# A twelve-layer perceiver on one core: layer 3 in three bfloat16 parts, unread products in layer 9, rows of norms between last steps

## The reference, cut to what matters

```
x = x + _L0_xattn_ref(_layernorm(x), ctx, ctx, ...)     # layer 1
x = x + _L0_attn_ref(_layernorm(x), ...)                # layer 2
x = x + _L0_ffn_ref(_layernorm(x), k0, k1, k2, s0, s1, s2)   # layer 3
...
x = x + _L2_ffn_ref(_layernorm(x), Wc, bc, W1, b1, W2, b2)   # layer 9
...
def _L0_ffn_ref(x, k0, k1, k2, s0, s1, s2):             # kernels are booleans: +1 or -1
    h = concatenate([x, -x])                            # 256 wide
    h = relu(s0 * (h @ pm1(k0))) * 2                    # 512 wide
    h = relu(s1 * (h @ pm1(k1))) * 2                    # 512 wide
    return s2 * (h @ pm1(k2))                           # 128 wide

def _L2_ffn_ref(x, Wc, bc, W1, b1, W2, b2):             # 32 experts x 4 sets, per batch of 32 rows
    logits = einsum('bntd,des->bntes', grouped, Wc) + bc + tie
    perm = (logits == max over the 32 rows)
    permuted = einsum('bntd,bntes->bnesd', grouped, perm)
    inner = relu(einsum('bnesd,esdf->bnesf', permuted, W1) + b1)
    result = einsum('bnesf,esdf->bnesd', inner, W2) + b2
    return einsum('bnesd,bntes->bntd', result, perm)
```

## Time and profile before

| | us |
|---|---|
| median of 3 runs | 3016.36 |
| lowest and highest | 3015.51, 3020.53 |
| the profiled execution, its own time | 3021.84 |
| its span in the trace | 3020.1 |
| PE busy | 2791.3 (92%) |
| DVE busy | 1734.3 (57%) |
| ACT busy | 1310.7 (43%) |
| POOL busy | 709.3 (23%) |
| layer 3, from the close of layer 2 to its own | about 743 to 836 |
| layer 9 | about 1461 to 1546 |

### The profile page before, as it was taken

How to read it: one execution, slowest core, us unless ns; L and a number is a source line. 1 busy time by engine, 2 the same in 40 slices (tenths; PEclk the granted TensorE clock), 3 DMA queues, 4 the chain that set the end, 5 groups by cost and what they waited for, 6 DMA issues and landing times.

```text
span 3020.1 us, 68763 instructions
## 1 busy us (share of the span) xinstructions
PE 2791.3 (92%) x26391; PEld 1793.0 (59%) x26391; DVE 1734.3 (57%) x5652; ACT 1310.7 (43%) x3546; POOL 709.3 (23%) x1552
## 2 busy tenths in 40 slices
PE   8999999897989979998689987789999999999898
PEld 7888885555467756665467765444444444444465
DVE  6778777665178877569558876722233232332544
ACT  4556564452278852348448874311121121111321
POOL 2444440000068850024027761000000000000000
PEclk9999999999999999888679998889999999999999
DMA  5111110000021110320011122040000000000000
GB/s 135 46 49 45 48 39 9 2 2 6 0 62 51 49 26 3 89 87 2 5 49 42 42 66 99 2 138 1 1 1 1 1 1 1 1 1 1 1 1 15
DMA packets 125902, 92.01 MB, mean 30 GB/s; under 512 B 41283, under 2 KB 122566, under 8 KB 124230
## 3 DMA queue, kind: packets, MB, share of 16 engines
q1 hardware_dynamic: 125574, 87.61, 10.2%
HBM read 83.89 MB, written 3.67 MB: 29 GB/s over the span
## 4 chain that ended last, share of the span: by engine, by line
PE 56%; DVE 8%; issue 6%; ACT 2%; DVEq 2%; POOLq 0%; POOL 0%; ACTq 0%
PE banks L3462 25%; PE banks L927 3%; PE banks L911 2%; PE banks L898 2%; PE banks L936 2%; PE banks L3885 2%; PE banks L3876 2%; PE banks L3874 2%; PE banks L3517 1%; PE banks L2390 1%; DVE probs L1099 1%; PE banks L900 1%; PE banks L3472 1%; PE banks L899 1%; PE banks L2006 1%
## 5 line engine op out<-in xcount | busy, mean ns | idle before, releaser
L1012 ACT ACTIVATE probs<-probs,nbias 128x257 f32<-128x257 f32 x512 | 254.4, 502 | 0.0
L1228 POOL TENSOR_SCALAR probs<-probs,rinv 128x257 f32<-128x257 f32 x512 | 238.5, 485 | 24.5 <-DVE rinv L1110 21.2
L3462 PE MATMUL banks<-Wz,hT 128*64 128x256 f32 x2048 | 226.4, 379 | 0.0
L3462 PE MATMUL banks<-Wn,hT 128*64 128x512 f32 x1024 | 225.4, 593 | 0.0
L3462 PE MATMUL banks<-Wr,hT 128*64 128x512 f32 x1024 | 225.2, 592 | 0.0
L3735 POOL COPY rb<-hT 128x512 f32<-128x512 f32 x32 | 35.8, 1118 | 801.5 <-ACT hT L3538 777.3
L3462 PEld LDWEIGHTS banks<-Wz,hT 128*64 128x64 f32 x2048 | 147.2, 137 | 87.5 <-issue 18.3
L3704 DVE TENSOR_TENSOR pr<-hb,banks 128x512 f32<-128x512 f32 x32 | 22.0, 688 | 298.3 <-PE banks L3517 298.3
L718 POOL TENSOR_SCALAR probs<-probs,rinv 128x257 f32<-128x257 f32 x256 | 120.6, 485 | 203.6 <-DVE rinv L658 203.0
L3462 PEld LDWEIGHTS banks<-Wr,hT 128*64 128x64 f32 x1024 | 73.6, 137 | 132.5 <-issue 127.9
L3462 PEld LDWEIGHTS banks<-Wn,hT 128*64 128x64 f32 x1024 | 71.0, 137 | 129.5 <-issue 129.5
(11 more groups left out here) (647 smaller groups left out, 6450.6 us busy)
## 6 DMA issues: line engine op xcount, KB each, us to landing
kvT<-in_ctx_T SPq DMA_DIRECT2D x192, 128.5 KB
kv<-in_ctx SPq DMA_DIRECT2D x64, 128.0 KB
kv<-in_ctx SPq DMA_DIRECT2D x32, 256.0 KB
W<-in_L_ffn_W_T SPq DMA_DIRECT2D x2, 2048.0 KB
Wr<-in_L_ffn_w_hh_T SPq DMA_DIRECT2D x1, 4096.0 KB
Wn<-in_L_ffn_w_hh_T SPq DMA_DIRECT2D x1, 4096.0 KB
Wz<-in_L_ffn_w_hh_T SPq DMA_DIRECT2D x1, 4096.0 KB
v_last<-v_last SPq DMA_DIRECT2D x192, 8.0 KB, 1.6
```

The source lines that it names most:

```text
L1012: i = e.activation(s, s, ACT.Exp, bias=self.nbias[v][:, r:r + 1], scale=self.scale, accum_out=self.rows_sum[v][:, r:r + 1])
L1228: e.tensor_scalar(s, s, self.rinv[v][:, r:r + 1], 1.0, ALU.mult, ALU.mult)
L3462: mm = e.matmul(self.bank[b][hf * BATCH:(hf + 1) * BATCH, 0:n], lhs, rhs, start=start, stop=stop, tile_position=(0, hf * BATCH))
```

## The change

Layer 3: the +1/-1 weights of the first two products become bfloat16, and each float32 operand is taken in three bfloat16 parts whose sum it is: its own upper half, read in place as every second 16-bit element (`high`); the upper half of what is left (`rest`, float32); and what is then left (`low`, bfloat16). DVE makes `rest` and `low` with two subtractions (`split`), for the turned rows (once a round) and for each of the four column groups of the first product's result. A call becomes three bfloat16 calls into one bank. The third product stays float32. The order on PE, ACT and DVE is written out anew: the first product of a round runs ahead of the second of the round before it, the third later; the last quarter's statistics stand ahead of the parts of the hidden rows, its rows between those of rounds 0 and 1.

Layer 9: the gathered columns are copied in one instruction for each bank (3 on ACT, 1 on DVE a group, 512 columns each); three float32 products of 512 columns into bank 6, which nobody reads, stand before the first pair, and one of 128 columns into bank 2 ahead of each `expert_pe`.

Layers 1, 7, 8: `next_rows` of quarters 0, 1, 2 go one by one between or behind the last steps.

```diff
-            if g == UN - 2:
-                for q in range(3):
-                    self.next_rows(e, q)
+            if g >= UN - 3:
+                self.next_rows(e, g - UN + 3)
...
+    FC, ROUNDS, TURN_BANKS, PARTS = 4, NT // 4, (0, 1, 2, 7), 3
...
-        self.W = [self.sb(f"W{n}", [P, c * wd]) for n, c, wd in ((0, 2, 512), (1, 4, 512), (2, 4, 128))]
+        self.W = [self.sb(f"W{n}", [P, c * wd], dt) for n, c, wd, dt in ((0, 2, 512, BF16), (1, 4, 512, BF16), (2, 4, 128, F32))]
         self.h = [[self.sb(f"h{n}", [P, FC * R4]) for n in range(2)] for _ in range(2)]
+        self.y_rest, self.y_low = [self.sb("y_rest", [P, R4]) for _ in range(2)], [self.sb("y_low", [P, R4], BF16) for _ in range(2)]
+        self.h_rest, self.h_low = [self.sb("h_rest", [P, FC * R4]) for _ in range(2)], [self.sb("h_low", [P, FC * R4], BF16) for _ in range(2)]
...
+        self.y_split, self.h_split = self.sig("y_split", N), self.sig("h_split", FC * N)
...
+    def high(self, t):
+        return t.bitcast(BF16).rearrange("p (n two) -> p n two", two=2)[:, :, 1]
+    def split(self, e, x, rest, low):
+        e.tensor_tensor(rest, x, self.high(x), ALU.subtract)
+        e.drain()
+        return e.tensor_tensor(low, rest, self.high(rest), ALU.subtract)
+    def parts(self, x, rest, low):
+        return self.high(x), self.high(rest), low
+
     def pe(self, e):
         self.norm_pe(e, (0, 1, 2))
+        self.first(e, 0)
+        self.first(e, 1)
+        self.second(e, 0)
+        self.norm_pe(e, (3,))
+        self.first(e, 2)
+        self.third(e, 0)
+        self.second(e, 1)
+        self.first(e, 3)
+        self.third(e, 1)
+        self.second(e, 2)
+        self.second(e, 3)
+        self.third(e, 2)
+        self.third(e, 3)
+    def first(self, e, r):
         self.signs_ready.wait_ge(e, 1)
+        self.y_split.wait_ge(e, r + 1)
+        at = slice(r * R4, (r + 1) * R4)
+        parts = self.parts(self.prog.yT[:, at], self.y_rest[r % 2][:, :], self.y_low[r % 2][:, :])
+        for c in range(self.FC):
+            self.n_yT.wait_ge(e, max(r, c % 2) + 1)
+            self.relu0.wait_ge(e, self.FC * r + c - 1)
+            for n, part in enumerate(parts):
+                i = e.matmul(self.bank[c % 2][:, :], self.W[0][:, c * P:(c + 1) * P], part, start=n == 0, stop=n == 2)
+            i.then_inc(self.mm0.up(), 1)
+    def second(self, e, r):
         FC = self.FC
...
+        self.signs_ready.wait_ge(e, 3)
+        self.n_yT.wait_ge(e, 3)
+        of = lambda t, k: t[r % 2][:, k * R4:(k + 1) * R4]
+        h0 = [self.h[n][0] for n in range(2)]
+        for c in range(FC):
+            self.relu1.wait_ge(e, FC * r + c - 1)
+            for k in range(FC):
+                self.h_split.wait_ge(e, FC * r + k + 1)
+                for n, part in enumerate(self.parts(of(h0, k), of(self.h_rest, k), of(self.h_low, k))):
+                    i = e.matmul(self.bank[2 + c % 2][:, :], self.W[1][:, k * 512 + c * P:k * 512 + (c + 1) * P], part,
+                                 start=k == 0 and n == 0, stop=k == FC - 1 and n == 2)
+            i.then_inc(self.mm1.up(), 1)
+    def third(self, e, r):
+        FC, h1 = self.FC, self.h[r % 2][1]
+        self.relu1.wait_ge(e, FC * (r + 1))
+        self.x_done.wait_ge(e, r - 1)
+        for s in range(4):
             for c in range(FC):
+                i = e.matmul(self.bank[4 + r % 2][:, s * P:(s + 1) * P], h1[:, c * R4 + s * P:c * R4 + (s + 1) * P],
+                             self.W[2][:, c * P:(c + 1) * P], start=c == 0, stop=c == FC - 1)
+        i.then_inc(self.mm2.up(), 1)
     def act(self, e):
...
+        self.relu_first(e, 0)
+        self.norm_act_std(e)
+        self.relu_first(e, 1)
+        self.relu_second(e, 0)
+        self.norm_act_yT(e, (3,))
+        self.relu_first(e, 2)
+        self.relu_second(e, 1)
+        self.relu_first(e, 3)
+        self.relu_second(e, 2)
+        self.next_root(e, 0)
+        self.next_root(e, 1)
+        self.relu_second(e, 3)
+        self.next_root(e, 2)
+    def relu_first(self, e, r):
+        FC, h0 = self.FC, self.h[r % 2][0]
+        for c in range(FC):
+            self.mm0.wait_ge(e, FC * r + c + 1)
+            self.mm1.wait_ge(e, FC * (r - 1))
+            self.h_split.wait_ge(e, FC * (r - 1))
+            e.activation(h0[:, c * R4:(c + 1) * R4], self.bank[c % 2][:, :], ACT.Relu, scale=self.scales[:, 0:1]).then_inc(self.relu0.up(), 1)
+    def relu_second(self, e, r):
+        FC, h1 = self.FC, self.h[r % 2][1]
+        self.signs_ready.wait_ge(e, 3)
+        self.mm2.wait_ge(e, r - 1)
+        for c in range(FC):
+            self.mm1.wait_ge(e, FC * r + c + 1)
+            e.activation(h1[:, c * R4:(c + 1) * R4], self.bank[2 + c % 2][:, :], ACT.Relu, scale=self.scales[:, 1:2]).then_inc(self.relu1.up(), 1)
+    def split_rows(self, e, r):
+        self.n_yT.wait_ge(e, r + 1)
+        self.mm0.wait_ge(e, self.FC * (r - 1))
+        self.split(e, self.prog.yT[:, r * R4:(r + 1) * R4], self.y_rest[r % 2][:, :], self.y_low[r % 2][:, :]).then_inc(self.y_split.up(), 1)
+    def split_hidden(self, e, r):
         FC = self.FC
...
+        self.mm1.wait_ge(e, FC * (r - 1))
+        for c in range(FC):
+            at = slice(c * R4, (c + 1) * R4)
+            self.relu0.wait_ge(e, FC * r + c + 1)
+            self.split(e, self.h[r % 2][0][:, at], self.h_rest[r % 2][:, at], self.h_low[r % 2][:, at]).then_inc(self.h_split.up(), 1)
+    def add_x(self, e, r):
+        x = self.prog.X[:, r * R4:(r + 1) * R4]
+        self.mm2.wait_ge(e, r + 1)
+        e.scalar_tensor_tensor(x, self.bank[4 + r % 2][:, :], self.scales[:, 2:3], x, ALU.mult, ALU.add).then_inc(self.x_done.up(), 1)
+        e.drain()
+        if r < 3:
+            self.next_statistics(e, r)
     def dve(self, e):
...
         e.tensor_scalar(self.W[0][:, :], self.raw[0][:, :], 2.0, -1.0, ALU.mult, ALU.add)
         e.drain()
         e.tensor_tensor(self.W[0][:, 0:512], self.W[0][:, 0:512], self.W[0][:, 512:1024], ALU.subtract).then_inc(self.signs_ready.up(), 1)
+        self.split_rows(e, 0)
         e.tensor_scalar(self.scales[:, 1:3], self.scales[:, 1:3], 2.0, None, ALU.mult).then_inc(self.signs_ready.up(), 1)
         for n in range(1, 3):
             e.tensor_scalar(self.W[n][:, :], self.raw[n][:, :], 2.0, -1.0, ALU.mult, ALU.add)
         e.drain().then_inc(self.signs_ready.up(), 1)
...
+        self.split_rows(e, 1)
+        self.norm_dve_statistics(e)
+        self.split_hidden(e, 0)
+        self.norm_dve_rows(e)
+        self.split_hidden(e, 1)
+        self.split_rows(e, 2)
+        self.split_hidden(e, 2)
+        self.add_x(e, 0)
+        self.split_rows(e, 3)
+        self.split_hidden(e, 3)
+        self.add_x(e, 1)
+        self.next_rows(e, 0)
+        self.next_rows(e, 1)
+        self.add_x(e, 2)
+        self.next_rows(e, 2)
+        self.add_x(e, 3)
...
         for step in range(NT + 5):
-            if step == NT + 3:
-                self.next_rows(e, 0)
-                self.next_rows(e, 1)
-            if step == NT + 4:
-                self.next_rows(e, 2)
...
             if t >= 0 and t % 4 == 3 and t < 12:
                 self.x_added.wait_ge(e, t + 1)
                 self.next_statistics(e, t // 4)
+            if step == NT + 1:
+                self.next_rows(e, 0)
+            if step == NT + 2:
+                self.next_rows(e, 1)
+            if step == NT + 4:
+                self.next_rows(e, 2)
...
                 if t > 4 and t % 4 == 1:
                     self.x_added.wait_ge(e, t - 1)
                     self.next_statistics(e, t // 4 - 1)
-                if t == NT - 2:
-                    for q in range(3):
-                        self.next_rows(e, q)
+                if t > NT - 4:
+                    self.next_rows(e, t - NT + 3)
 
     def rotary(self, e, t, b, ts, bs, bank):
         bq = lambda t: t.rearrange("p (b q) -> p b q", q=SEQ)
...
                         i = e.matmul(bank[2 + b][:, at], p.y[lo:lo + SEQ, g * R4 + s * P:g * R4 + (s + 1) * P],
                                      self.pick_tok[g % 2][lo:lo + SEQ, at], start=True, stop=True)
                 i.then_inc(self.gather_mm.up(), 1)
+        self.keep_warm(e, bank[6][:, :], 3)
         self.G_dve.wait_ge(e, 4)
         self.G_act.wait_ge(e, 4)
...
+    def gathered(self, g, b):
+        return self.G3[:, :, 16 * g:16 * g + 16].rearrange("p x (s b) -> p x s b", b=BPT)[:, :, :, b]
+    def keep_warm(self, e, bank, times):
+        for _ in range(times):
+            e.matmul(bank, self.prog.ones[:, :], self.prog.y[:, 0:bank.shape[1]], start=True, stop=True)
+
...
     def expert_pe(self, e, n):
+        self.keep_warm(e, self.bank[2][:, 0:P], 1)
         self.inner_ready.wait_ge(e, n + 1)
         self.G_back.wait_ge(e, n)
         for k in range(2):
...
             if phase == 2:
                 self.gather_mm.wait_ge(e, g + 1)
                 for b in (1, 2, 3):
-                    for s in range(4):
```

(21 more changed lines are left out.)

44 lines of the change are left out of this document (1 added, 43 removed).

## The result

The changed kernel takes 3001.03 us (median of 4 runs, 2995.86 to 3001.28), the kernel before 3018.18 beside it: a ratio of 0.9931, 95% interval 0.9910 to 0.9953, or -20.8 us (-27 to -14). In six more runs on another chip it is 0.9922 (0.9901 to 0.9944), -23.6. The profiled execution has its own time of 3000.97 and a span of 2999.2, against 3021.84 and 3020.1.

The account below looks back on a forecast made before the run. PE's turns bound layer 3; PE and DVE waiting on each other at half clock bound layer 9's pairs. -15.5 - 0.4 + 1.5 - 7.8 - 0.6 - 1.5 - 0.9 = -25.2 us: 2996.6, median 5.5 lower, 2991.2; range 2983 to 3005.

Parts of the forecast that it names:

- rival 1: Layer 9: PE's clock falls back in the pairs, unread products wake nothing; -14.6 us in all, 3001.8; chance 0.26.
- the start of the pairs: Layer 9 before the first pair: regrouped copies -0.4 us for four groups, three unread products +1.5 us.
- the pairs: Layer 9's loop: clock held at 1.00, period 1.52 instead of 2.02 us, -7.8 us; first `inner_pe` another -0.6.
- the spread part: Layer 9 behind the pairs: the raised clock lasts into it, where it was at half clock; -1.5 us.
- the rows: Rows moved between last steps: layer 1 -0.3, layer 8 -0.6, layer 7 0 us; -0.9 in all.
- Layer 3, the products: Three bfloat16 parts cost 0.651 us a call, not 0.869; second product saves 13.9 us, first about 1.3.
- rival 3: Layer 3: reads of every second 16-bit element go at half rate, layer 3 +14.6 us; 3027 in all; chance 0.07.
- Layer 3, order and start: Layer 3 as a whole, by a hand timeline of the new order and DVE's splits: -15.5 us (-18 to -12).
- 3.1 of stalls: Layer 3: PE's 0.78 us wait for the last Relu before each third product goes, once a round; 3.1 us.
- The timeline: Layer 3: first product at 746.4, PE full from 765.2, last add at 819.2 instead of 835.22.
- Rival 2: Layer 9: regrouped copies are quick as well, -4.2 us more, -29.9 in all, 2986.5; chance 0.12.
- Rival 4: Layer 3's gains are covered by something unseen, as DVE held up by both operands; about 3013; chance 0.05.

Follow-up runs that it names:

- l3_order: Changed kernel with layer 3 in its new order but in float32, without splits: -13.0 us (-18 to -8) against the kernel before.
- more_unread: Changed kernel plus unread products before the first turn of seven layers and ahead of layer 9's spread part: -1.8 us (-7 to +3) against the kernel before.
- no_unread: Changed kernel without any unread product in layer 9: -23.9 us (-31 to -17) against the kernel before.
- no_unread_again: Changed kernel without any unread product in layer 9, run once more: -23.3 us (-30 to -17) against the kernel before.
- l9_only: Kernel before with only layer 9's copies and unread products changed: -12.1 us (-18 to -6) against the kernel before.
- no_three: Changed kernel without the three unread 512-column products ahead of layer 9's pairs: -17.2 us (-24 to -11) against the kernel before.

## Why the prediction was right, and where it was not

The forecast was 2991 with -25.2 us; it came to 3001, with -20.8 and -23.6. Faster was right, and inside layers 3 and 9 so was the mechanism. The number is no witness for it: rival 1's 3001.8 lies nearer to 3001.03 than the forecast, and only the period of 1.57 at clock 1.00 rules it out. Nor does the near sum: layer 3 and the start of the pairs came out some 2.5 us better than forecast, the pairs, the spread part and the rows 3.1 worse, and these cancel.

- **Layer 3, the products.** A bfloat16 record turns every 0.227 us on `h`, 0.225 on `h_rest` and 0.215 on `h_low`, so a call takes 0.667 where 0.651 was forecast (13.9 + 1.3 = 15.2 for both products forecast, 13.2 measured by l3_order). The parts read at a step are 5% slower than the dense one, so rival 3 (0.33 and above) is out. Here a page of the Trainium skill (Advanced Engine Details and Errata, SBUF Cachelines) agrees to within these 5%: its two hits on a line are met by a step of one element in 4 bytes.
- **Layer 3, order and start.** -15.5 forecast, -16.9 measured. The order alone gave 3.7, where 3.1 of stalls were counted. A split is 0.75 + 0.61 = 1.36 (1.37 forecast). The timeline held: with the 3.6 added by which it was ahead, the trace of after has the first product at 746.8 (746.4 by hand), the first split of `h` at 750.8 (751.2), the last add at 818.35 (819.2). Too much were those 0.85 at the end and the 0.5 that I took off for a start at half clock.
- **Layer 9, copies and the three.** The copies take 0.95 each, as forecast; -0.16 a group against -0.1. Rival 2 is out. Copies and products together were to make the first pair 1.1 later in its layer; it is 0.1 earlier by ACT's first `inner` and 0.1 later by PE's records (1475.79 + 14.41 = 1490.20 against 1490.06). In the traces without the three it is 0.5 to 0.7 earlier, so they cost about 0.6 and not 1.5. By the forecast's own terms 1486.9 + 4.4 is 1491.3 and not 1491.5; and the three took 3.9, most of it beside ACT's copies (until 1474.9), which I had not set against them.
- **Layer 9, the pairs and the first `inner_pe`.** -8.4 forecast with a period of 1.52, -7.2 measured with 1.57 (ACT's first `inner` 14.5 early, its first `rb` 21.65). Rival 1 is what happens without the three, and after four pairs without the product in the pairs.
- **Layer 9, the spread part.** This is the step that failed: -1.5 forecast, 0 measured. I took the clock to last into it; PE idles 0.48 ahead of the last `expert_pe` and 0.81 behind it, and the first turns are at 0.50 (1504 to 1508). more_unread put products there and won 1.6.
- **Rows.** -0.9 forecast, -0.5 measured: -0.19, +0.3, -0.59.
- **From the sum to the time.** The local terms come to -16.9 - 7.2 - 0.5 = -24.6, near the -25.2. The 10 us between 2991 and 3001 are elsewhere. I took 5.5 off because the median of three runs lay that far below the profiled execution's own time; with more executions the kernel before had medians of 3018.2 to 3020.7, which leaves 1.2 to 3.7 of it. And the other stretches of a single trace move by several us, as the table shows. Rival 4's 3013 has no working: with layer 3 at nothing and the rest as forecast, 25.2 - 15.5 = 9.7 us under 3016.4 are 3006.7.
- **What the sum left out.** It adds what layer 9 saves to the whole. no_unread and no_unread_again say that within the changed kernel 6.6 us of it are not seen at the end: their mean is no higher, and layers 10 and 11 are 9 us shorter in their traces than in the changed kernel's. Only l9_only (-12.1, -18 to -6, against the kernel before) shows a gain at the end.

Open: by what layers 4 to 8 and 10 to 11 differ between kernels and executions, why layers 10 and 11 take back what layer 9 gains within the changed kernel, and whether the change makes the losses in layers 4 to 8 likelier. No run varied the place of the instructions in memory, or anything else that a changed line moves besides its own work.

## What to carry to other kernels

A product that is bound by TensorE's turns and needs float32's precision can go in three bfloat16 parts, read in place by a stride: 0.67 us for 512 columns in place of 0.87, if VectorE has 1.4 us a tile to spare. Where a loop waits on another engine at half clock, unread products are worth a try, but both are needed, some to wake the engine and some to keep it awake, and they belong in front of the wait that makes the idle time. Take them out again and look at the whole time: here they took 6.6 us off their layer and no slower kernel was measured without them. And compare stretches between marks before crediting a change with a trace's whole difference: here code that nobody had touched moved by 9 us.

## What the hardware did that I had not expected

- PE at 0.50 with records open in 36.00 of 36.00 us (no_three), while in the changed kernel the clock rose to 0.96 within the three products of 512 columns.
- The same code, layers 10 and 11, came out between -8.5 and +0.9 us in different kernels, and the same to 0.3 us in two executions of one (no_unread -8.0 and -8.3, the changed kernel +0.8 and +0.9).
- The first 20 us came out either 0 or 3.0 us later than in the kernel before, in lines that are the same (3.0 in the changed kernel, -0.2 in changed_again).
